# A selective scan with its projections on one core: eight products split 12 to 4 passes around a transposition, state saved in pairs, three small jobs moved by a slot

## The reference

```python
skip = resid_norm @ W_skip                      # 512 -> 1024
x_in = resid_norm @ W_in                        # 512 -> 1024
x = _silu(conv(x_in, 4 taps) + conv_b)
delta = softplus(x @ W_delta_1 @ W_delta_2 + b_delta_2)
Bm, Cm = x @ W_B, x @ W_C                       # 16 states
h = h * exp(delta * A) + (delta * x) * B_l      # along the tokens, for 1024 channels x 16 states
y = sum over the states of h * C_l
out = resid + ((y + x * W_D) * _silu(skip)) @ W_out
```

## Time and profile before

| | |
|---|---|
| median of 3 runs | 2221.14 us (2216.73 to 2223.62) |
| the profiled execution, its own time | 2224.15 us |
| span of its instructions | 2222.4 us |
| busy, PE | 1895.3 us, 85% |
| busy, PE's weight loads | 1586.4 us, 71% |
| busy, DVE | 1751.9 us, 79% |
| busy, ACT | 1715.9 us, 77% |
| busy, POOL | 1859.3 us, 84% |
| mean granted TensorE clock | 0.959 of 2.4 GHz |

### The profile page before, as it was taken

How to read it: one execution, slowest core, us unless ns; L and a number is a source line. 1 busy time by engine, 2 the same in 40 slices (tenths; PEclk the granted TensorE clock), 3 DMA queues, 4 the chain that set the end, 5 groups by cost and what they waited for, 6 DMA issues and landing times. The chain is left out here.

```text
span 2222.4 us, 35976 instructions
## 1 busy us (share of the span) xinstructions
PE 1895.3 (85%) x12005; PEld 1586.4 (71%) x12005; DVE 1751.9 (79%) x2785; ACT 1715.9 (77%) x3404; POOL 1859.3 (84%) x1256
## 2 busy tenths in 40 slices
PE   4677777998989898998889899898889888888783
PEld 4566666878777776878778786877778776767551
DVE  3487878898898888898888888889898888888422
ACT  3479797988889797988879796988879797888321
POOL 1389998898989898998989998998989899999312
PEclk9889898999999999999999999999999999999996
DMA  5656566675756575675747576665657466645310
GB/s 172 217 171 199 174 197 211 218 233 176 250 167 233 183 252 177 218 232 181 235 139 269 178 227 210 213 219 181 226 168 266 144 193 214 203 157 181 104 57 19
DMA packets 234675, 425.95 MB, mean 192 GB/s; under 512 B 18622, under 2 KB 134906, under 8 KB 234490
## 3 DMA queue, kind: packets, MB, share of 16 engines
q1 hardware_dynamic: 234490, 423.65, 58.5%
HBM read 339.18 MB, written 84.41 MB: 191 GB/s over the span
## 5 line engine op out<-in xcount | busy, mean ns | idle before, releaser
L613 POOL TENSOR_TENSOR hc<-h,c_all 128x1024 f32<-128x1024 f32 x512 | 1204.5, 2364 | 126.5 <-DVE h L971 113.7
L971 DVE TENSOR_TENSOR_SCAN h<-operand,carry,bank 128x512 f32<-128x512 f32 x528 | 658.1, 1272 | 148.2 <-PE bank L1143 119.3
L747 ACT ACTIVATE u_t<-dx_t,lbc 128x256 f32<-128x256 f32 x1408 | 632.1, 498 | 51.3 <-PE bank L1143 51.3
L1143 PE MATMUL bank<-ident,u_t 128*128 128x128 f32 x2816 | 445.8, 282 | 204.8 <-DVE h L971 201.6
L1148 PE MATMUL y_sum<-ident,hc 128*128 128x128 f32 x4096 | 598.8, 277 | 7.2 <-POOL hc L613 6.6
L1143 PEld LDWEIGHTS bank<-ident,u_t 128*128 128x128 f32 x2816 | 341.3, 145 | 340.7 <-issue 238.9
L1148 PEld LDWEIGHTS y_sum<-ident,hc 128*128 128x128 f32 x4096 | 489.0, 143 | 52.1 <-issue 36.7
L728 ACT ACTIVATE operand<-delta_q,neg_a 128x512 f32<-128x512 f32 x704 | 479.9, 711 | 0.0
L728 ACT ACTIVATE bank<-delta_q,neg_a 128x512 f32<-128x512 f32 x320 | 218.7, 683 | 231.8 <-DVE h L971 230.6
L597 POOL TENSOR_TENSOR operand<-dx_q,b_all 128x1024 f32<-128x1024 f32 x160 | 378.4, 2365 | 9.1 <-DMA b_all<-bc_dram 9.1
L971 DVE TENSOR_TENSOR_SCAN h<-bank,carry,operand 128x512 f32<-128x512 f32 x240 | 294.8, 1270 | 14.9 <-POOL operand L597 10.7
(11 more groups left out here) (119 smaller groups left out, 1898.4 us busy)
## 6 DMA issues: line engine op xcount, KB each, us to landing
c_all<-bc_dram SPq DMA_DIRECT2D x256, 512.0 KB, 4.4
b_all<-bc_dram SPq DMA_DIRECT2D x160, 256.0 KB, 5.5
win<-in_L_attn_W_in SPq DMA_DIRECT2D x64, 512.0 KB, 6.0
wskip<-in_L_attn_W_skip SPq DMA_DIRECT2D x64, 512.0 KB, 6.5
x_dram<-x SPq DMA_DIRECT2D x64, 256.0 KB, 6.2
delta_dram<-delta SPq DMA_DIRECT2D x32, 512.0 KB, 7.6
dx_dram<-dx SPq DMA_DIRECT2D x32, 512.0 KB, 5.4
delta_q<-delta_dram SPq DMA_DIRECT2D x32, 512.0 KB, 6.0
```

What stands on the lines that cost most here:

```text
L613: nc.gpsimd.tensor_tensor(hc[:, number % 3], h[:, number % 3], c_all[:, j % 2, s % 2:s % 2 + 1].to_broadcast([P, 2, SPAN]), ALU.mult).then ...
L747: last = nc.scalar.activation(u_t[:, j % 2, b], dx_t[:, k, b], ACT.Copy, scale=lbc[:, stage % 2, b, DELTA + n:DELTA + n + 1])
L971: nc.vector.tensor_tensor_scan(h[:, number % 3, q], first, second, start, ALU.mult, ALU.add).then_inc(scan_done.sem, 1)
L1143: last = transpose(bank[:, q, b * P:(b + 1) * P], u_t[:, j % 2, b, q * P:(q + 1) * P], ident[:])
```

## The change

It has five parts. The 16 passes of a pair's in- and skip-projection are issued 12 behind the second turn and 4 between the turns, instead of 8 and 8 (`CUT`). The carries of two slots are saved by one instruction in even slots, behind the scan that follows the two; `carry` has another layout, and the two slots' places in it depend on which buffers of h they had (`carry_place`). The `wlbc` products of pairs 0, 1 and 2 move from between the turns of slots 11, 12 and 13 to behind the second turn of slots 11, 12 and 14. The output projection of block 1 moves from behind the second turn to between the turns in slots 0 to 7. The moments of o move from the route job's slot 40 to 41, that is from slot 8 to 9.

```diff
+PIECES = [(e, k) for e in range(2) for k in range(KD)]
+CUT = PIECES[:6], PIECES[6:]
...
-        carry = sb("carry", P, N, ET)
+        carry = sb("carry", P, N // 2, 2, ET)
...
-        carry_saved = signal("carry_saved", "scan", SLOTS)
+        carry_saved = signal("carry_saved", "scan", SLOTS // 2)
...
-                    if v := due(dve, carry_saved, t, s - 1):
+                    if v := due(dve, carry_saved, t, (s - 1) // 2):
                         dve.wait_ge(carry_saved.sem, v)
...
-                        start = 0.0 if stage % STAGES_PER_BATCH == 0 else carry[:, n, et:et + 1]
+                        start = 0.0 if stage % STAGES_PER_BATCH == 0 else carry[:, n // 2, carry_place(number - 2 * SLOTS), et:et + 1]
...
-                def save_carry(t, s):
+                def carry_place(number):
+
+                    return number % 2 ^ (number // 2 * 2 % 3 == 2)
+
+                def save_carries(t, s):
+
                     if not (now := slot_of(t, s)):
                         return
                     t, s = now
                     _, quarter, n, _, number = place(t, s)
-                    if v := due(dve, scan_done, t, 2 * (s + 1)):
+                    if v := due(dve, scan_done, t, 2 * (s + 2)):
                         dve.wait_ge(scan_done.sem, v)
-                    copied(carry[:, n, 2 * quarter:2 * quarter + 2],
-                           h[:, number % 3, :, SPAN - 1]).then_inc(carry_saved.sem, 1)
+                    first = number % 3
+                    both = h[:, 0:3:2] if first == 2 else h[:, first:first + 2]
+                    copied(carry[:, n // 2, :, 2 * quarter:2 * quarter + 2],
+                           both[:, :, :, SPAN - 1]).then_inc(carry_saved.sem, 1)
...
-                        save_carry(step, slot - 1)
+                        if slot % 2 == 0:
+                            save_carries(step, slot - 2)
...
-                                    if v := due(dve, nz_ready, t - 1, 1):
-                                        dve.wait_ge(nz_ready.sem, v)
+                                    for read in (nz_ready, var_o):
+                                        if v := due(dve, read, t - 1, 1):
+                                            dve.wait_ge(read.sem, v)
                                     moments(z, mvz, var_z)
...
-                                if s == 40:
+                                if s == 41:
                                     if v := due(dve, o_ready, t, TB):
                                         dve.wait_ge(o_ready.sem, v)
                                     moments(o, mvo, var_o)
...
                                 if (s, late) in ((TAPPED[p] - 3, 1), (TAPPED[p] - 2, 0)):
-                                    e = s - TAPPED[p] + 3
...
-                                    for k in range(KD):
+                                    for e, k in CUT[1 - late]:
                                         last = matmul(pair_bank(p)[:, e * T:(e + 1) * T],
                                                       win[:, p % 2, k, e * P:(e + 1) * P],
                                                       rnt[:, k, :], start=(k == 0), stop=(k == KD - 1))
-                                    last.then_inc(in_done.sem, 1)
-                                if s == (11, 12, 13, 15)[p] and not late:
+                                        if k == KD - 1:
+                                            last.then_inc(in_done.sem, 1)
+                                if (s, late) == ((11, 1), (12, 1), (14, 1), (15, 0))[p]:
...
                                 if (s, late) in ((3 * p + 13, 1), (3 * p + 14, 0)):
-                                    e = s - 3 * p - 13
...
-                                    for k in range(KD):
+                                    for e, k in CUT[1 - late]:
                                         last = matmul(routed[:, e * T:(e + 1) * T],
...
-                                    if e:
+                                    if not late:
                                         last.then_inc(skip_done.sem, 1)
...
-                            if 26 <= s < 30 or (32 <= s < 32 + ET and late):
+                            if 26 <= s < 30 or (32 <= s < 32 + ET and not late):
```

## The result

The changed kernel takes 2245.91 us (median of 4 runs, 2245.34 to 2248.28) where the kernel before, beside it on the same chips, takes 2218.93: ratio 1.0125, 95% interval 1.0098 to 1.0152. It is 27 us slower; 14.5 were forecast. The time lies in the stated range of 2207 to 2250, near its upper end.

The account below looks back on a forecast made before the run. The bound was taken as a chain alternating between PE and DVE, no engine being full. Terms 17.3 + 17.8 - 6.7 - 9.1 - 4.8 gave +14.5 us on 2221.1, so 2236 us; range 2207 to 2250.

Parts of the forecast that it names:

- second rival: POOL sets the step's length from scan 15 on, so charges are absorbed and credits are not: 2205 us; chance 0.15.
- The split, 0: Splitting passes 12 to 4 moves 0.86 us from the second turn's wait to the first's; cost 0.
- first rival: The split shortens the chain, four waits a step losing 0.86 us each: 48 us, giving 2187; chance 0.05.
- Output products, +17.3: Block 1's output projection between the turns, slots 0 to 7: 1.33 us lost in each of 13 steps, +17.3 us.
- The terms at slots 1 and 5: Output products of slots 0 and 4 delay the second turns for slots 1 and 5: 0.47 and 0.86 us lost.
- the products of slots 2 and 3 stay inside their stretch: Moving the output products of slots 2 and 3 between the turns costs 0.
- Those of 5 and 7 fall into DVE's work: 0: Output products of slots 5 and 7, moved between the turns, cost 0 because they fall into DVE's work.
- Moments, +17.8: Last moments moved from slot 8 to 9: all 1.48 us of DVE exposed in 12 steps, +17.8 us.
- Carries, -6.7: Saves after slots 1, 5, 9, 25 and 21 leave the chain: 0.42 us in 16 steps, -6.7 us.
- wlbc, -9.1: wlbc products behind the turn end scan 12's second-half wait in slot 11: mean -0.65 us in 14 steps, -9.1 us.
- the odd steps, -4.8: Scan 15 ends earlier, so slot 28's dx_q load comes about 0.8 us earlier in 6 steps: -4.8 us.
- the fourth rival: Longer PE idling ahead of slot 11 brings 1.2 GHz in all steps: 7 to 9 us more, 2245; chance 0.2.

Follow-up runs that it names:

- e1: The changed kernel with the moments of o back in slot 8 (route job's slot 40): 2229.4 us, ratio 1.0048 to the kernel before.
- e2: The changed kernel with the output projection of block 1 back behind the second turn: 2223.8 us, ratio 1.0022 to the kernel before.
- e10: The changed kernel with moments, output projection and wlbc products as before, leaving carries in pairs and the split: 2214.0 us, ratio 0.9989 to the kernel before.
- e9: The changed kernel with moments, output projection and the 8 and 8 split as before, leaving carries and wlbc products: 2204.9 us, ratio 0.9944 to the kernel before.
- e4: The changed kernel with moments back in slot 8 and output projection back behind the second turn: 2201.8 us, ratio 0.9931 to the kernel before.
- e7: The changed kernel with only slot 4's output product back behind the second turn: 2240.8 us, ratio 1.0109 to the kernel before.
- e6: The kernel before with the carries in pairs alone: 2215.1 us, ratio 0.9993 to the kernel before.
- e12: e4 with slot 0's output product alone moved between the turns: 2218.2 us, ratio 1.0014 to the kernel before.
- e8: The changed kernel with the output products of slots 2 and 4 back behind the second turn: 2241.2 us, ratio 1.0105 to the kernel before.
- e13: e1 with slot 0's output product alone back behind the second turn: 2225.1 us, ratio 1.0032 to the kernel before.

## Why the prediction was right, and where its sizes were off

**The direction and the chain: right.** The time lies in the range and on the forecast side. The stretches between PE's fresh starts, read from the trace before, told where a moved instruction counts: the moments cost in slots 9 and 10 (e1, e2), the products between turns in slots 1 and 5 (e1, the traces), the wlbc products pay in slot 11 (e10), and the split is neutral (e9), with 0.86 us going from the one wait to the other at slot 5 as forecast, and 0.7 to 0.9 at slots 21 and 24 (e9, e4). POOL did not decide (second rival): DVE waited 12.7 us for its operand before and 11.1 after.

**The split, 0: right.** The most regular wait of the trace, 1.35 us, could not be shortened by moving work behind the turn before it, since PE had no gap in between. The first rival is out.

**Output products, +17.3: mis-sized.** Measured 27.6 without the moments' move and 22.1 with it (the change minus e2). The terms at slots 1 and 5 hold together (0.53 and 0.78 against 0.47 and 0.86). The failed step is "the products of slots 2 and 3 stay inside their stretch": the product in slot 2 costs 1.6 us whenever it runs at the low clock, since the second turn of slot 3 had no room even at the high one. The two halves of scan 3 start 1.13 us apart in steps 8 and 9 of the kernel before; in the changed kernel it is 1.16 in step 8, at the high clock, and 2.84 in step 9, at the low one. In steps 11 and 12 of e1, where the low clock stayed away from slot 2, the way from slot 0 to 10 is 1.19 and 1.29 us longer than in e4, near the forecast 1.33; in the other eight of the steps 4 to 13 it is 2.6 to 3.4. "Those of 5 and 7 fall into DVE's work: 0" failed too, but adds little to the sum: slot 5's product does delay scan 6 (e7), which takes from slot 4's product most of the 0.86 it was charged, and of slot 7's 0.41 as much comes back at slots 8 to 10 (0.53).

**Moments, +17.8: right**, 16.5 with the output products moved and 22.0 without, the 1.48 us a step measured as 1.33 to 1.46. Twelve times 1.45 are 17.4; the profiled executions of e2 and e4 differ by 18.8, and where the rest of the 22.0 lies was not found.

**Carries, -6.7: wrong**, -0.9 (e6), not to be told from 0. What failed is the list of slots that were taken to lie on the chain: e6 against the kernel before shows 0.23 us gained from slot 6 to 8 and 0.18 lost again from 8 to 10 (the second half of scan 9 waits 0.69 us for PE in step 8, before 0.49), 0.13 gained from 16 to 18 and 0.14 lost to 20, where scan 19 waits for ACT's decays, 1.30 us in both. DVE reaches a place where another engine is the bound a little earlier and waits there. I had applied that to the moments and not to the saves.

**wlbc, -9.1, and the odd steps, -4.8: near in sum (-12.2), not shown in the parts.** From slot 10 to 16 e4 is 0.95 us a step shorter than e10, some 13 us in 14 steps (an estimate from steps 3 to 13). So the wlbc term was too small, and nothing is left for the odd steps: from slot 28 to 30 they are not shorter in e4 than in e10, but longer by 0.6 in the mean of six, in a scatter of 2 us. That the two errors cancel is luck.

**The low clock (the fourth rival, 0.2): its condition came true, its price lay elsewhere.** Of the steps 3 to 13, the low clock begins in slots 10 to 12 in six before, in seven in e4, and in all eleven in the changed kernel and in e2, where PE idles longer ahead of slot 11's turn (2.89 us in step 8). That the idle time alone does it is not shown: e12, with 1.44 us there, has it in all eleven too. And e2 needs only 0.13 us a step more than e4 from slot 10 to 12, where 7 to 9 us in all were priced; that the moved wlbc products no longer delay a turn there is the likely reason, and was not tested apart. Most of the cost is where the low clock met a product between two turns, at slots 2 to 4. So the rival's 2245, next to the 2245.9 measured, is luck. Rows 14 are also read wrongly: the second window covers slot 9 to the start of slot 11 of step 10 and ends just ahead of that step's low clock. From 1391 to 1401 us the granted clock is 0.83, so step 10 had the low clock as step 9 did; that it comes in about half of the steps holds all the same.

The forecast sum of the two costs, 35.1 us, was 44.1; that of the gains, 20.6, was 16.7 (e4). The two misses, 9.0 and 3.9, add up to the 12.5 us between 14.5 and 27 within what can be told. The direction was earned; the size was low by nearly a half.

**A better kernel.** e4, the change without its output projection and moments parts, takes 2201.8 us, ratio 0.9931 (0.9911 to 0.9950) to the kernel before and 44 us below the changed one.

## What to carry to other kernels

Cut the trace at the places where an engine that ran without a gap waits again for another one; between two such places only the bounding engine's sum counts, not the order of its work. A wait that stands in every slot is then no promise: ask whether the work moved out of it lands ahead of the next wait on the same engine. And a change in several parts wants a run of each part taken out: here two lost 44 us and hid a gain of 17.

## What was not expected of the hardware

- The granted TensorE clock reacts to small shifts. In e4 and e1 PE idles 1.50 and 2.10 us ahead of slot 3; behind it the clock stays high in e4 and is low in e1 in eight of the eleven steps 3 to 13. But e12 idles the same 2.10 us and keeps the high clock in nine of them. What beside that idle time decides was not settled.
- The low clock seems to be met somewhere once the step has more idle time: taking a product away from where it was met moved the cost to later slots (e8) or the low clock itself (e13); the time at the low clock was 133 us in the changed kernel, 126 in e8, and 116 in e13 against 126 in e1.
- A reduction of four values per partition costs DVE 133 ns and one of two 130: its size is free here, its count is not, and yet the 256 saved instructions brought nothing.
